# Moving the expert blocks, the operand loads and the small row transfers of a fused two-layer kernel

## The reference

```
xn = layernorm(x)                                   # layer 0 has been added to x before
q, k, v = split(xn @ qkv_w.T + qkv_b)               # 16 heads of 16 features
scores  = q k^T / 4 + slope_h * (j - i), causal     # 2048 x 2048 per head
s = softmax(scores) v @ out_w.T + out_b
logits = xn @ gate_w.T + gate_b                     # 8 experts, the best 2 of each token
for e in range(8):                                  # w1: 512 x 256, w2: 256 x 256
    h = xn @ w1[e].T + b1[e]
    y = h_even * sigmoid(1.702 h_even) * (h_odd + 1)
    ffn += (y @ w2[e].T + b2[e]) * weight_of(e)
x = x + s * silu(ffn)
```

## Time and profile before

| what | value |
|---|---|
| median of 3 runs (lowest to highest) | 820.03 us (818.52 to 823.14) |
| the profiled execution | 815.3 us |
| its span, first to last instruction | 813.5 us |
| mean granted clock of TensorE | 0.938 of full speed |
| busy: PE, DVE, ACT, POOL | 678.5, 601.9, 475.5, 279.3 us |

### The profile page before, as it was taken

One profiled execution on the slowest core, in us unless ns is written; L12 is line 12 of the kernel. 1 busy time (PEld: TensorE's weight loads), 2 busy tenths in 40 slices (PEclk: granted clock), 3 DMA queues, 4 the chain that ended last, 5 costly groups with the idle time before them and its releaser, 6 DMA issues.

```text
span 813.5 us, 14740 instructions
## 1 busy us (share of the span) xinstructions
PE 678.5 (83%) x5306; PEld 312.0 (38%) x5306; DVE 601.9 (74%) x1222; ACT 475.5 (58%) x990; POOL 279.3 (34%) x458
## 2 busy tenths in 40 slices
PE   3478859769889888989898898889898989898885
PEld 1234545433233433444344444443443443232432
DVE  5999776689777786787678777867886788688342
ACT  2276685860566575666565665666565656666551
POOL 2313442027723323333323433233333234660112
PEclk9889889985899999999999999999999999799998
DMA  9710324634450453244233323522442221350001
GB/s 293 251 65 0 97 73 160 200 130 149 161 145 1 124 152 87 71 124 125 72 86 127 93 74 111 148 83 79 134 127 72 80 90 46 88 185 14 27 32 47
DMA packets 76852, 85.84 MB, mean 106 GB/s; under 512 B 34169, under 2 KB 60284, under 8 KB 76412
## 3 DMA queue, kind: packets, MB, share of 16 engines
q1 hardware_dynamic: 71114, 74.05, 30.0%
q0 software_dynamic: 3280, 8.98, 3.5%
q10 hardware_dynamic: 2386, 1.87, 0.8%
HBM read 39.54 MB, written 27.53 MB: 82 GB/s over the span
## 4 chain that ended last, share of the span: by engine, by line
PE 55%; ACT 18%; DVE 13%; issue 7%; ACTq 3%; DMA 2%; SPq 1%; POOL 1%; POOLq 0%; DVEq 0%
PE bank L1575 16%; ACT PR L830 11%; PE bank L1511 9%; PE bank L1469 8%; DVE PM L1233 5%; PE bank L1534 5%; PE bank L1483 4%; PE bank L1341 3%; ACTq L811 3%; PE bank L1589 2%; PE bank L1384 2%; PE bank L1614 2%; ACT TG L788 1%; ACT U L819 1%; DMA qk_parts<-TG 1%
## 5 line engine op out<-in xcount | busy, mean ns | idle before, releaser
L830 ACT ACTIVATE PR<-bank 128x512 f32<-128x512 f32 (+3 forms) x640 | 317.1, 537 | 226.0 <-PE bank L1534 127.4
L1233 DVE TENSOR_REDUCE PM<-bank 128x1 f32<-128x512 f32 (+3 forms) x640 | 354.3, 604 | 73.6 <-PE bank L1511 46.4
L1534 PE MATMUL bank<-OPS 57*128 57x512 f16 (+3 forms) x640 | 209.6, 363 | 53.4 <-ACT PR L830 48.3
L1511 PE MATMUL bank<-OPS 54*128 54x512 f16 (+3 forms) x640 | 195.8, 372 | 10.5 <-DVE PM L1233 7.0
L1575 PE MATMUL bank<-PR,VS 128*17 128x512 f32 (+3 forms) x1280 | 161.2, 556 | 0.0
L1511 PEld LDWEIGHTS bank<-OPS 54*128 54x128 f16 x640 | 50.2, 95 | 129.6 <-DVE PM L1233 86.9
L1534 PEld LDWEIGHTS bank<-OPS 57*128 57x128 f16 x640 | 54.0, 94 | 117.6 <-ACT PR L830 109.1
L1469 PE MATMUL bank<-WB 128*128 128x256 f16 x552 | 81.2, 277 | 0.0
L600 POOL CAST POSB<-YT 128x256 f16<-128x256 f32 x46 | 18.2, 396 | 173.8 <-DVE YT L1135 173.8
L1469 PEld LDWEIGHTS bank<-WB 128*128 128x128 f16 x552 | 48.2, 98 | 32.5 <-issue 25.9
L1544 PE MATMUL bank<-MASK 64*128 64x64 bf16 x512 | 59.5, 199 | 0.0
(11 more groups left out here) (185 smaller groups left out, 893.2 us busy)
## 6 DMA issues: line engine op xcount, KB each, us to landing
WB<-W SPq DMA_DIRECT2D x23, 512.0 KB, 3.6
OPS<-qk_parts SPq DMA_DIRECT2D x60, 192.0 KB
x_rows<-PR SPq DMA_DIRECT2D x23, 256.0 KB, 3.3
WB<-in_w SPq DMA_DIRECT2D x23, 256.0 KB, 3.5
y_rows<-XT SPq DMA_DIRECT2D x23, 256.0 KB, 3.0
W<-in_w SPq DMA_DIRECT2D x6, 512.0 KB, 5.7
XT<-in_b SPq DMA_DIRECT2D x23, 128.0 KB, 3.9
XO<-in_x SPq DMA_DIRECT2D x4, 512.0 KB, 13.0
```

The costliest lines, as they stand in the source:

```text
L830: act.activation(PR[:, tile % RING, off:CH], PS[2 + tile % 2][:, off:CH], ACT.Exp, scale=1 / SCORE).then_inc(b_exped, 1)
L1233: dve.tensor_reduce(PM[:, c % 2, j, xq, gg:gg + 1], bank[:, 0:width], AX.X, ALU.max).then_inc(a_reduced, 1)
L1511: last = mm(bank[:, 0:width], OPS[ROWS_A, slot, 0, P * (TC * a + xq):P * (TC * a + xq) + P], OPS[ROWS_A, slot, 1, CH * gg:CH * gg + width] ...
L1534: last = mm(bank[:, off:CH], OPS[ROWS_B, slot, 1, P * k:P * k + P], OPS[ROWS_B, slot, 0, CH * b + off:CH * b + CH], start=True, stop=k < T ...
```

## The change

1. Blocks begin at step 76, alternately 20 and 24 steps apart, always at a multiple of 4 (`values` stands at n % 4 == 2). A half's `up` goes as two groups of six (steps n, n + 4 and n + 12, n + 16) in place of three matmuls in each of four steps. `down` of a block moves to step n + 8 of the next one, the last to 588 (it was 552). Gate, split and gather steps follow; in DVE's list a block's `expert_out` now stands behind the joining of a chunk's heads.
2. `fetch_block` is issued 26 steps ahead in place of 20, without the biases, which get their own `fetch_biases` 10 steps ahead.
3. `load` becomes `load_half`: per pair four parts at steps 4, 24 (A rows), 48 and 68 (B rows) of the pair, the A rows of pair p + 1 as soon as the A-tiles of pair p - 1 are done, its B rows as soon as the B-tiles of that pair are. Before the loop only the A rows of heads 2 and 3 are loaded.
4. `rows_out` moves from ACT to SP, with the same two transfers, at the same step of SP's loop.
5. Some semaphores are joined. The turns and `heads_out` move by up to two steps, so that all bank 7 work stands at n % 4 == 0.

```diff
-FIRST_BLOCK, EVERY = 92, 20
+FIRST_BLOCK, EVERY = 76, 22
...
-TURN_AT = {chunk_end(m) - 1 + (17, 17, 11, 5)[m] if m < NC else chunk_end(m) - 1 + 5: m for m in range(NC * PAIRS)}
-HEADS_AT = {chunk_end(m) - 1 + LEAD + 11: m for m in range(NC * PAIRS)}
+TURN_AT = {chunk_end(m) + ((16, 16, 8, 4)[m] if m < NC else 4): m for m in range(NC * PAIRS)}
+HEADS_AT = {chunk_end(m) + LEAD + 12: m for m in range(NC * PAIRS)}
+BLOCK_AT = {FIRST_BLOCK + EVERY * b // 4 * 4: b for b in range(BLOCKS)}
+UP_AT = {n + 12 * f + 4 * part: (b, f, part) for n, b in BLOCK_AT.items() for f in range(2) for part in range(2)}
+TANH_AT = {n + 11 * f + 6: (b, f) for n, b in BLOCK_AT.items() for f in range(2)}
+GATE_AT = {n + 10 * f + 7: (b, f) for n, b in BLOCK_AT.items() for f in range(2)}
...
+DOWN_AT = {n + 8: b - 1 for n, b in BLOCK_AT.items() if b}
+DOWN_AT[max(BLOCK_AT) + 28] = BLOCKS - 1
+FETCH_AT = {n - 26: b for n, b in BLOCK_AT.items()}
+FETCH_BIAS_AT = {n - 10: b for n, b in BLOCK_AT.items()}
+LOAD_AT = {PER_PAIR * p + at: (2 * p + 2 + r, half) for p in range(PAIRS - 1)
+           for half, r, at in ((0, 0, 4), (0, 1, 24), (1, 0, 48), (1, 1, 68)) if p or half}
...
-GATHER_AT = {PER_PAIR * (PAIRS - 1) + 4 + 4 * n: n for n in range(NT)}
+GATHER_AT = {TOTAL - 40 + 3 * n: n for n in range(NT)}
...
+            def load_half(h, half):
+
+                p = h // 2 - 1
+                if p:
+                    sp.wait_ge((a_scored, b_scored)[half], PER_PAIR * p)
+                if half and h % 2 == 0:
+                    wait(sp, opb_in, 16 * 2 * 3 * p)
+                done = opb_in if half else opa_in[h // 2 % 2]
+                load_rows(h, half, done)
+                load_parts(h, half, slice(0, S), done)
...
-            load(2)
-            load(3)
+            load_half(2, 0)
+            load_half(3, 0)
...
             for n in range(STEPS):
+                if n - 2 in TURN_AT:
+                    rows_out(TURN_AT[n - 2])
                 if n in FETCH_AT:
                     fetch_block(FETCH_AT[n])
+                if n in FETCH_BIAS_AT:
+                    fetch_biases(FETCH_BIAS_AT[n])
                 if n - 1 in STORE_AT:
                     store_block(STORE_AT[n - 1])
-                p, rest = divmod(n - LEAD - 1, PER_PAIR)
-                if rest == 0 and 1 <= p < PAIRS - 1:
-                    sp.wait_ge(b_scored, PER_PAIR * p)
-                    load(2 * p + 2)
-                if rest == 8 and 1 <= p < PAIRS - 1:
-                    load(2 * p + 3)
+                if n in LOAD_AT:
+                    load_half(*LOAD_AT[n])
...
-            def rows_out(m):
-
-                p, a = m // NC, ORDER[m % NC]
-                act.wait_ge(mt_copied, m + 1)
...
-                for f in range(2):
-                    for t in range(4):
-                        if n - t - 9 * f in BLOCK_AT:
-                            for j in range(3 * (t % 2), 3 * (t % 2) + 3):
-                                up(BLOCK_AT[n - t - 9 * f], f, t // 2, j)
+                if n in UP_AT:
+                    for j in range(6):
+                        up(*UP_AT[n], j)
```

More of the change, by code:

```diff
@@ L450, in fetch_block, with fetch_biases, rows_out @@
                 sp.dma_start(W2B[par].unsqueeze(1), w2[:, ds(e, 1), :, :]).then_inc(block_in[par], 16)
-                sp.dma_start(B2B[:, par, :], b2[ds(e, 1), :].broadcast_to([P, D])).then_inc(block_in[par], 16)
-                sp.dma_start(BB[:, par, :, :].unsqueeze(1), B1S[:, ds(e, 1), :, :]).then_inc(block_in[par], 16)
                 sp.dma_start_transpose(XB[par].rearrange("p j k n -> p (j k) n"),
                                        x_rows[SLOTS * b:SLOTS * b + SLOTS, :]).then_inc(block_in[par], 16)
+            def fetch_biases(b):
+                par = b % 2
+                if b >= 2:
+                    sp.wait_ge(ye_copied, b - 1)
+                if b == 0:
+                    sp.wait_ge(b1_prep, 3)
+                wait(sp, biases_in, 32 * b)
+                e = sp.value_load(EXPERT[0:1, b:b + 1], min_val=0, max_val=E - 1)
+                sp.dma_start(B2B[:, par, :], b2[ds(e, 1), :].broadcast_to([P, D])).then_inc(biases_in, 16)
+                sp.dma_start(BB[:, par, :, :].unsqueeze(1), B1S[:, ds(e, 1), :, :]).then_inc(biases_in, 16)
+            def rows_out(m):
+                p, a = m // NC, ORDER[m % NC]
+                sp.wait_ge(mt_copied, m + 1)
+                for j in range(2):
+                    sp.dma_start(OPS[ROWS_MAX, (2 * p + j) % 4, 0, CH * a:CH * a + CH].rearrange(
+                        "j (q t) -> j q t", q=TC), MT[3 * TC * j:3 * TC * j + 3 * TC, m % 2, :]).then_inc(mrow[m % NC], 16)
             def store_block(b):
@@ L804, in max_rows @@
                 act.activation(MT[:, m % 2, :], MTP, ACT.Copy, scale=1 / UNIT).then_inc(mt_copied, 1)
-            def rows_out(m):
-                p, a = m // NC, ORDER[m % NC]
-                act.wait_ge(mt_copied, m + 1)
-                for j in range(2):
-                    act.dma_start(OPS[ROWS_MAX, (2 * p + j) % 4, 0, CH * a:CH * a + CH].rearrange(
-                        "j (q t) -> j q t", q=TC), MT[3 * TC * j:3 * TC * j + 3 * TC, m % 2, :]).then_inc(mrow[m % NC], 16)
             def chunk_out(m):
@@ L1293, in _ @@
                     sort(n + EXPERTS_KNOWN - 4)
-                for f in range(2):
-                    if n - 6 - 9 * f in BLOCK_AT:
-                        glu(BLOCK_AT[n - 6 - 9 * f], f)
-                    if n - 7 - 9 * f in BLOCK_AT:
-                        linear(BLOCK_AT[n - 7 - 9 * f], f)
-                if n - 1 in DOWN_AT:
-                    expert_out(DOWN_AT[n - 1])
+                if n in GLU_AT:
+                    glu(*GLU_AT[n])
+                if n in LINEAR_AT:
+                    linear(*LINEAR_AT[n])
                 if n in ADD_AT:
@@ L1528, in score_b @@
                     pe.wait_ge(b_exped, tile - 1)
+                if tile % PER_PAIR == 0:
+                    wait(pe, opb_in, 16 * 2 * 3 * p)
                 if tile % PER_PAIR == OFF[c]:
```

46 lines of the change are left out of this document (22 added, 24 removed).

## The result

The changed kernel takes 824.04 us (median of 14 runs, 818.54 to 830.54), the kernel before 818.43 in the runs beside it (815.83 to 823.14). The ratio is 1.006, 95% interval 1.0034 to 1.0086: slower by 0.6%, where I had forecast 810 us. The profiled execution took 818.54 us, its span 816.7; the trace of before had 815.3 and 813.5.

What follows compares the result with a forecast made beforehand. The prediction saw a chain of waits alternating between PE and ACT, with no engine full. Terms of -12, -23, +13.5, +7 and +4 us sum to -10.5, from 820.0 to 809.5, said as 810; range 788 to 838.

Steps and rivals of the forecast that it cites:

- rows at pair borders: Chunk 3's row transfers where head pairs meet, late behind the next pair's load where SP is held: +4 us, bounds 0 to 14.
- Rows of chunks 0 and 2: Start of attention: chunk 0's rows wait behind loads, +13.5 us; chunk 2's behind the fetch of block 0, +7 us.
- two rules that I weighed: SP's queue at B-tile 0: transfers of SP and ACT interleave (0 us), or each issuer's ring goes in order (13.5 us).
- Row transfers off ACT: Issue of row transfers leaves ACT's list, where it delayed exponentials: -12 us, bounds 24 us gained and 0.
- blocks spread: Expert blocks' matmuls, one group per pair of scores: 2.8 us per block in place of 3.8, -23 us, bounds -78 to +6.
- forecast stretch of 69 us: Steady attention: 80 tiles with 3.6 blocks were to take about 69 us in place of 75.5.
- Rival 1: Attention: the score chain is the bound and a block still costs 3.8 us; 838 us, chance 0.25.
- rival 2: Start of attention: small transfers pass the loads, so chunk 0 is on time; 799 us, chance 0.12.
- rival 3: Expert blocks nearly hidden, at 1.6 us each: -50 us from spreading, 783 us, chance 0.08.
- rival 4: Whole kernel: score chain fills the gaps ACT's issues leave, gains and waits cancel within 4 us; 820 us, chance 0.10.
- At no price: gathers later: End of attention: gathers from step 600 on, done by POOL under the last 40 steps, cost nothing; 1 to 3 us if they slip.

Runs made afterwards that it cites:

- neither part: Changed kernel with ACT issuing the row maxima, blocks by the tables of before, and a pair's first load at step 8: 823.72 us, ratio 1.0058 to the kernel before.
- both orders altered: Changed kernel with first chunks' row maxima between and ahead of the loads of heads 2 and 3, and a pair's first load at step 8: 769.58 us, 0.9414.

## Why the prediction was wrong, point by point

By ratios the change falls into four steps, each between two kernels of one chain, so that they add up to the measured 0.6% of themselves. ACT's issue and the spread give -53 us, the borders +36, the front +17, and what the kernel with neither part has above before is +5. I had -35, +4, +20.5 and 0.

*The step that failed: rows at pair borders, +4 with bounds 0 and 14.* It measured 36. I took 7 us for the load and 5.7 us of slack, 1.3 us short, and charged 2 to 3 us only where a fetch holds SP (and the upper bound has seven borders; six have such a load). Two things were missing. The slack was counted at the old rate while the change made steps shorter: six steps of the new 64.30 / 80 are 4.8 us. And the load isn't alone: at the second and the fifth border block weights go out just ahead of it, and with the waits PE ran at 1.2 GHz for a while, to which I put most of some 10 us beyond the 22.7.

*Cause of that wait.* I had taken it for order on SP's queue. At the front and where a fetch held SP that holds: with ACT issuing, the waits went or nearly so. At the first four borders it doesn't: the rows came late from ACT's queue too, beside a load issued before them. That load kept three engines' worth busy; that the rows ran on the same ones is not shown, but with the load spread over more engines those waits went down to 0.25 us at most. The order alone (36 us) or the width of the loads alone (40 us, front included) removes most of it. I had priced the load's bytes by its rate, 62 GB/s (1.72 MB in 27.6 us), and not asked why it was so low while weights move at 300.

*Rows of chunks 0 and 2, +20.5.* The places were right, to 0.3 us at B-tile 0 and to 2 us at B-tile 24; the end felt 17, since with both orders altered PE still waits 2.33 us for the rows and 2.25 for block 0's token rows. Of the two rules that I weighed, both are seen. By the Trainium skill's "Issuing engines are not separate DMA queues" ("DMA: Bandwidth & Descriptors") transfers of SP and ACT interleave, and a second issuing engine saves issue time only. The trace agrees with the first half: ACT's rows passed while SP's load was still running, within 6.6 to 6.8 us of their issue. It doesn't agree with the second half at the front: B-tile 0 waited 14.53 us for row maxima on SP's queue, behind the loads, and none for those on ACT's. There the order within one queue decided, as the forecast had it.

*Row transfers off ACT (-12) and blocks spread (-23).* Alone they gained 21 us each, the spread near its forecast and the issue above it, and together 53. I added them as if independent. The forecast stretch of 69 us matches the spread alone (69.20); with both it is 64.30. Rival 1 (a block's cost stays) is refuted by this, rival 2 (the small transfers pass the loads) by B-tile 0. On this stretch rival 3 (blocks nearly hidden, 1.6 us each) came nearest: 64.30 is 3.9 us above the 60.4 of 80 tiles without a block, 1.1 us for each of 3.6 blocks, though the 60.4 still hold ACT's issues. The time is nearest to rival 4's 820, but not by its way: gains of 53 us met costs of 58.

*At no price: gathers later.* Steps 644 to 683 became 6.4 us longer (51.50 to 45.10). Putting the gathers early, with blocks closer, gave 4.5 us back in the trace; putting six of the sixteen gather steps behind the maxima gave 1.5. PE is busy 4.3 us longer there at clock 0.87, so most of it is PE's pace. The +5 above lies there too: with neither part the same steps take 53.9 us at clock 0.78.

```profile
744.20:798.10 53.90, 46.68 (x223) 19.13 (x225) 19.57 (x36) 25.47 (x54) 13.29 (x14) 0.78 0.11 36
```

Why the clock falls there was not settled; late gathers are common to these kernels, but with the same gathers it was 0.87 in one and 0.78 in another.

## What to carry to other kernels

A transfer of a few KB that something waits for can be late by a bulk load issued before it, also from another queue: put it ahead of the load, or cut the load so that it spreads over more engines. When a change makes steps shorter, every slack counted in steps shrinks in us: recount it at the new rate. Two parts that relieve the same pair of engines may each gain little alone, so price them together.

## What the runs showed of the hardware

A load of 48 partitions whose source has an outer size of 3 went at 66 to 82 GB/s on three engines' worth of busy time (a share of 0.19 of 16); the same bytes as three transfers of 16 partitions passed in 3.4 us in place of 6.2. Beside such loads, a transfer of 3 KB from another engine's queue was through 6.6 to 6.8 us after its issue, at the front and at a border alike. Each of five waits of PE of 2.3 to 7.8 us at a border came with 3.4 to 10.2 us at 1.2 GHz; without the waits the clock stayed at 2.4 GHz for 457 us. A wait for a transfer is not needed for such a fall: the kernel before has five of 3.4 us between 248 and 628 us, where PE waits for none.
